# Cross attention in a decoder layer: where the weights are transposed and the values multiplied

## The reference, cut to what matters

```python
x = x + attn(layernorm(x), ...)
q = (queries @ Wq + bq)      # 16 heads of 64, queries = layernorm(x)
k = (keys @ Wk + bk)         # 154 context rows per batch
v = (values @ Wv + bv)
att = einsum('bhqd,bhkd->bhqk', q, k) / 8
att = att * attention_weights            # fside
att = where(attention_mask, -inf, att)
att = softmax(att)
out = einsum('bhqk,bhkd->bhqd', att, v)
x = x + (out @ Wo + bo)
x = x + ffn(layernorm(x), ...)           # top 2 of 8 experts, and a shared one
```

## Time and profile before

| | us |
|---|---|
| median of three runs | 585.82 |
| runs | 584.96 to 586.62 |
| profiled execution, first to last instruction (span) | 582.9 |
| TensorE busy | 562.7 |
| VectorE busy | 441.9 |
| ScalarE busy | 326.0 |
| GpSimd busy | 233.1 |

### The profile page before, as it was taken

One profiled execution on the slowest core, in us unless ns is written; L12 is line 12 of the kernel. 1 busy time (PEld: TensorE's weight loads), 2 busy tenths in 40 slices (PEclk: granted clock), 3 DMA queues, 4 the chain that ended last, 5 costly groups with the idle time before them and its releaser, 6 DMA issues.

```text
span 582.9 us, 11123 instructions
## 1 busy us (share of the span) xinstructions
PE 562.7 (97%) x3656; PEld 426.1 (73%) x3656; DVE 441.9 (76%) x838; ACT 326.0 (56%) x1005; POOL 233.1 (40%) x228
## 2 busy tenths in 40 slices
PE   8999999999999999999999999999999999999991
PEld 6547566788697978888788787878777776666661
DVE  3999999999886879958688679866677555656650
ACT  3632424368869796795976939715223245455220
POOL 1110110307580834387234671625235333353443
PEclk9999999999999999999999999999999999999997
DMA  8930004162741231423316107892645443344323
GB/s 301 347 101 2 1 1 172 45 217 91 274 155 65 100 119 45 173 74 93 127 37 218 65 20 230 270 390 87 181 111 90 67 64 58 53 70 61 54 29 35
DMA packets 36183, 68.37 MB, mean 117 GB/s; under 512 B 5504, under 2 KB 29024, under 8 KB 33632
## 3 DMA queue, kind: packets, MB, share of 16 engines
q1 hardware_dynamic: 28208, 57.99, 29.7%
q0 software_dynamic: 6784, 8.95, 9.5%
q10 hardware_dynamic: 1136, 0.73, 0.4%
HBM read 56.62 MB, written 15.25 MB: 123 GB/s over the span
## 4 chain that ended last, share of the span: by engine, by line
PE 58%; DVE 18%; DMA 9%; issue 7%; POOL 3%; ACT 2%; POOLq 1%; SPq 0%; DVEq 0%
PE pb L744 9%; PE pb L636 6%; DVE R L1140 6%; PE pb L499 6%; PE pb L601 6%; PE pb L549 6%; DMA out_dram<-R 5%; PE pb L565 5%; PE pb L778 5%; PE pb L516 4%; PE pb L648 3%; DVE R L1163 3%; DMA x<-in_x_dram 2%; DMA out_dram<-R,hidx 2%; PE pb L569 2%
## 5 line engine op out<-in xcount | busy, mean ns | idle before, releaser
L896 ACT ACTIVATE R<-R,mx 128x154 f32<-128x154 f32 x256 | 104.4, 415 | 0.2
L1761 POOL DMA_INDIRECT out_dram<-R x36 | 55.8, 1549 | 80.3 <-DMA out_dram<-R 33.9
L744 PE MATMUL pb<-R 128*128 x256 | 81.0, 459 | 0.0
L1022 ACT ACTIVATE R<-R 128x352 f32<-128x352 f32 x36 | 17.9, 497 | 91.6 <-DVE R L1572 80.3
L744 PEld LDWEIGHTS pb<-R 128*128 128x128 f32 x256 | 46.2, 190 | 20.4
L499 PE MATMUL pb<-xnT,wq 128*128 128x256 f32 x256 | 58.2, 383 | 0.0
L887 ACT ACTIVATE R<-pb,bq 128x256 f32<-128x256 f32 x64 | 30.1, 474 | 47.9 <-PE pb L499 47.8
L499 PEld LDWEIGHTS pb<-xnT,wq 128*128 128x128 f32 x256 | 47.7, 190 | 7.8 <-issue 1.2
L908 ACT COPY R<-pb 128x512 f32<-128x512 f32 x80 | 40.8, 614 | 18.4 <-PE pb L549 18.3
L1685 POOL DMA_INDIRECT xs_dram<-xn,pos x32 | 31.8, 993 | 47.3 <-DVE pos L1324 39.0
L896 ACT ACTIVATION_READ_ACCUMULATOR R<-R,mx 128x1 f32 x256 | 49.5, 193 | 0.0
(11 more groups left out here) (202 smaller groups left out, 1180.1 us busy)
## 6 DMA issues: line engine op xcount, KB each, us to landing
R<-in_fside_dram SPq DMA_DIRECT2D x16, 1232.0 KB, 5.5
R<-in_L_ffn_w_dram SPq DMA_DIRECT2D x16, 352.0 KB
R<-in_mask_dram SPq DMA_DIRECT2D x16, 308.0 KB, 2.9
R<-xs_dram SPq DMA_DIRECT2D x32, 129.0 KB, 2.1
KV<-in_ebias_dram SPq DMA_DIRECT2D x2, 1440.0 KB
out_dram<-x SPq DMA_DIRECT2D x4, 512.0 KB, 4.7
R<-in_L_ffn_w_dram SPq DMA_DIRECT2D x8, 256.0 KB, 4.5
x<-in_x_dram SPq DMA_DIRECT2D x3, 512.0 KB, 11.4
```

The lines of the kernel that those rows point to most:

```text
L744: ins = e.matmul(pb[:, u.i, 0:F], xsT[:, s % 2, k, :], ew13[:, bass.ds(w_reg[s] * 1408 + q * 704 + k * F, F)], start=(k == 0), stop=(k == 1))
L896: ins = e.activation(att[t % 3][:, h, :], att[t % 3][:, h, :], ACT.Exp, bias=mx[:, a4, 1, h:h + 1], accum_out=mx[:, a4, 2, h:h + 1])
L1761: e.indirect_dma_start(out=out, out_offset=bass.IndirectOffsetOnAxis(ap=to.bitcast(U32), axis=0), in_=rows, in_offset=None, compute_op=ALU ...
```

## The change

In passes 2 to 7 all 40 transposes of a unit's weights follow each other, and the value products of both halves are made in one go into four banks instead of two times four: half 0 goes to columns 0 to 255 and half 1 to 256 to 511 of the same bank. VectorE reads the four banks with two operations of 1024 elements instead of four of 512, and `combined` takes its blocks in the order 0, 1, 4, 5, 2, 3, 6, 7. The queries of the next unit are split: blocks 0 to 3 before the transposes, 4 and 5 between transposes and product, 6 and 7 behind the product and `turned`. ScalarE's order follows. In pass 7, which has no queries, the second block of `shared_out` stands between transposes and product. Pass 1 is as before, as is the last unit's work behind pass 7.

```diff
@@ -571,6 +571,40 @@
                         if r % 2:
                             ins.then_inc(full[u.i], 1)
 
+            def product_whole(u8):
+                b = u8 // 4
+                uses = [u for g in range(2) for u in bank.take_pair(("av", u8, g))]
+
+                def turned_in(hf, n):
+                    d = bank["pT", u8, hf, n // 2]
+                    w.wait_ge(free[d.i], d.drained)
+                    return pT[:, hf, n, :]
+
+                for hf in range(2):
+                    cols = slice(256 * hf, 256 * hf + 256)
+                    for n in range(8):
+                        u, to = uses[n // 2], 64 * (n % 2 ^ n // 4)
+                        w.wait_ge(free[u.e], u.empty)
+                        e.matmul(pb[to:to + 64, u.i, cols], vm[b][:, 8 * hf + n, :], turned_in(hf, n),
+                                 start=(hf == 0), stop=False)
+                for hf in range(2):
+                    cols = slice(256 * hf, 256 * hf + 256)
+                    for g in range(2):
+                        for r in (0, 2, 1, 3):
+                            u, to = uses[2 * g + r // 2], 64 * (r % 2 ^ g)
+                            ins = e.matmul(pb[to:to + 64, u.i, cols], vr[b][32 * r:32 * r + 32, 2 * hf + g, :],
+                                           turned_in(hf, 8 + g)[32 * r:32 * r + 32, :], start=False, stop=(hf == 1))
+                            if hf and r % 2:
+                                ins.then_inc(full[u.i], 1)
+
+            def weights_all_turned(u8):
+                for n in range(3):
+                    d = bank["con", B - 1, n]
+                    w.wait_ge(free[d.i], d.drained)
+                for hf in range(2):
+                    for k in range(5):
+                        weights_turned(u8, hf, k)
+
             def values(u8, between, amid=None, turning=None):
                 for n in range(3):
                     d = bank["con", B - 1, n]
@@ -595,8 +629,8 @@
                 for q in range(2):
                     u = bank.take(("wo", u8, q))
                     w.wait_ge(free[u.e], u.empty)
-                    for j in range(8):
-                        d = bank["av", u8, j // 4, j // 2 % 2, 0]
+                    for j in (0, 1, 4, 5, 2, 3, 6, 7):
+                        d = bank["av", u8, j // 2 % 2, 0]
                         w.wait_ge(free[d.i], d.drained)
                         ins = e.matmul(pb[:, u.i, 0:D], oT[:, j, q * P:(q + 1) * P], wo[:, j, :],
                                        start=(j == 0), stop=(j == 7))
@@ -689,12 +723,21 @@
                 scores(u8)
                 if u8 == 1:
                     queries(2, range(7))
+                    values(0, None, None, lambda: queries(2, range(7, 8)))
                 elif u8 < 7:
-                    queries(u8 + 1)
+                    queries(u8 + 1, range(0, 4))
+                    weights_all_turned(u8 - 1)
+                    queries(u8 + 1, range(4, 6))
+                    if u8 in (4, 6):
+                        place(u8 // 2 - 2)
+                    product_whole(u8 - 1)
+                    if u8 in BETWEEN:
+                        turned(*BETWEEN[u8])
+                    queries(u8 + 1, range(6, 8))
                 else:
-                    shared_out(*FILL[6])
-                values(u8 - 1, BETWEEN.get(u8), (lambda: place(u8 // 2 - 2)) if u8 in (4, 6) else None,
-                       (lambda: queries(2, range(7, 8))) if u8 == 1 else None)
+                    shared_out(*FILL[6], lambda: weights_all_turned(6))
+                    product_whole(6)
+                    turned(*BETWEEN[7])
                 if u8 - 1 in FILL and u8 < 7:
                     shared_out(*FILL[u8 - 1])
                 if gating is not None:
@@ -900,7 +943,7 @@
 
             def evacuate(u8, hf, lo, hi):
                 for i in range(4 if u8 else 0):
-                    d = bank["av", u8 - 1, hf, i // 2, i % 2]
+                    d = bank["av", u8 - 1, hf, i // 2, i % 2] if u8 == 1 else bank["av", u8 - 1, i // 2, i % 2]
                     w.wait_ge(full[d.i], d.filled)
                 for k in range(lo, hi):
                     u = bank["pT", u8, hf, k]
@@ -970,19 +1013,28 @@
             for u8 in range(1, NU):
                 t0, t1 = 2 * u8, 2 * u8 + 1
                 gating = u8 >= 3 and u8 % 2
-                if u8 < 7:
-                    queries(u8 + 1, range(7 if u8 == 1 else 8))
-                evacuate(u8 - 1, 0, 0, 5)
                 if u8 == 1:
+                    queries(2, range(7))
+                    evacuate(0, 0, 0, 5)
                     queries(2, range(7, 8))
-                evacuate(u8 - 1, 1, 0, 3)
-                if u8 in BETWEEN:
-                    normalise(*BETWEEN[u8])
-                if u8 not in BETWEEN:
+                    evacuate(0, 1, 0, 3)
                     exps(t0, range(0, 2))
-                evacuate(u8 - 1, 1, 3, 5)
-                if u8 in BETWEEN:
-                    turned(*BETWEEN[u8])
+                    evacuate(0, 1, 3, 5)
+                else:
+                    if u8 < 7:
+                        queries(u8 + 1, range(0, 4))
+                    evacuate(u8 - 1, 0, 0, 5)
+                    evacuate(u8 - 1, 1, 0, 5)
+                    if u8 < 7:
+                        queries(u8 + 1, range(4, 6))
+                    if u8 in BETWEEN:
+                        normalise(*BETWEEN[u8])
+                    else:
+                        exps(t0, range(0, 2))
+                    if u8 in BETWEEN:
+                        turned(*BETWEEN[u8])
+                    if u8 < 7:
+                        queries(u8 + 1, range(6, 8))
                 if u8 == 7:
                     exps(t0, range(0, 8))
                     exps(t0, range(8, 16))
@@ -1250,6 +1302,20 @@
                     e.tensor_tensor(oT[:, j:j + 2, :], pb[:, u.i:u.i + 2, 0:256],
                                     bvT[:, j:j + 2].rearrange("p (j a) -> p j a", a=1).broadcast_to([P, 2, 256]),
                                     ALU.add).then_inc(free[u.i], 1)
+
+            def product_whole(u8):
+                w.wait_ge(in_bv, 16)
+                d = bank["wo", u8 - 1, 1]
+                w.wait_ge(full[d.i], d.filled)
+                for g in range(2):
+                    u, v = bank["av", u8, g, 0], bank["av", u8, g, 1]
+                    w.wait_ge(full[u.i], u.filled)
+                    w.wait_ge(full[v.i], v.filled)
+                    e.tensor_tensor(
+                        oT[:, :, :].rearrange("p (f b) q -> p f b q", f=2)[:, :, 2 * g:2 * g + 2, :],
+                        pb[:, u.i:u.i + 2, :].rearrange("p b (f q) -> p f b q", f=2),
+                        bvT[:, :].rearrange("p (f b a) -> p f b a", f=2, a=1)[:, :, 2 * g:2 * g + 2, :].broadcast_to(
+                            [P, 2, 2, 256]), ALU.add).then_inc(free[u.i], 1)
 
             def attended(u8, qs=(0, 1)):
                 w.wait_ge(xbo.sem, xbo[u8])
@@ -1424,15 +1490,18 @@
                 for hs in heads_of(t0):
                     top(t0, hs)
                     if hs == (0, 8):
-                        product(6, 0)
+                        product_whole(6)
                 mask(t1, (0, H))
-                if u8 < 7:
-                    product(u8 - 1, 0)
+                if u8 == 1:
+                    product(0, 0)
                 if u8 in (4, 6):
                     place(u8 // 2 - 2)
                 if u8 < 7:
                     top(t1, (0, H))
-                product(u8 - 1, 1)
+                if u8 == 1:
+                    product(0, 1)
+                elif u8 < 7:
+                    product_whole(u8 - 1)
                 if gating is not None:
                     logits(gating)
                 if u8 == 7:
```

## The result

The changed kernel takes 597.43 us, the median of five runs (596.68 to 599.65), against 585.82 for the kernel before: a ratio of 1.0209, 95% interval 1.0192 to 1.0225. By the medians it is slower by 11.6 us. The forecast was 597.2.

A forecast was written before the change was run, and what follows sets the result against it. Two nearly equal bounds: TensorE's own work, and a loop ScalarE, VectorE, GpSimd, TensorE. Shifts through the passes reach +11.4: 582.9 + 11.4 = 594.3 us of span, plus 2.9 to the median, 597.2; range 589 to 601.

The forecast's parts named there:

- TensorE's work: Value products on TensorE, passes 2 to 7: fewer changes to 32-row tiles, -0.35 us a pass, -2.1 over six.
- Half 1 too early for GpSimd: Transposes wait for GpSimd's scaled second half: 1.4 us in pass 2, 1.4 in pass 3 (part earlier), 1.05 in pass 6.
- ScalarE's start: Exponentials stand behind queries 6 and 7: 1.9 us later every pass by order alone, 3.3 in pass 2 with its wait.
- Banks: TensorE waits for VectorE's first product operation to free banks: gate in pass 3 about 1.0 us, `shared_out` in pass 4 1.7.
- Pass 5: -0.35 us, then the gate chain again as in pass 3: a shift of +7.2 us at the scores of pass 6.
- Pass 7, the step that failed: VectorE's whole product comes between the halves of `top`, +11.6 us; +11.4 from the transposes of weights 7 to the end.
- Span to median: Whole kernel: the median of the runs lies 2.9 us above the profiled span, taking 594.3 to 597.2 us.
- Rival (a): Only ScalarE's order and pass 7 bite, no waits for scaled halves or banks: +5.7, 591.5 us; chance 0.21.
- Rival (c): Mask and `scale` swap order in passes 2 and 6, GpSimd takes 1.90 us, not 4.38: 594.8 us; chance 0.12.
- Rival (b): TensorE is the bound everywhere, hand-overs stay hidden, only row-tile changes count: -2.1, 583.7 us; chance 0.06.

The follow-up runs named there:

- the memsets: Changed kernel with three small memsets on VectorE before the even tile's mask in passes 2 and 6: 598.05 us, ratio 1.0218.
- the first experiment: Kernel before the change with only `turned` moved behind the second value product, so ScalarE's exponentials start 2.5 us later: 593.16 us, ratio 1.0127.
- queries 0 to 5: Changed kernel with query blocks 0 to 5 all ahead of the transposes: 594.99 us, ratio 1.0155.
- pass 7 with both blocks first: Changed kernel with both blocks of `shared_out` ahead of the 40 transposes in pass 7: 595.45 us, ratio 1.0165.

## Why the prediction was right, and where it was not

The mechanism and the size were right: 597.2 against 597.43, span +11.4 against +12.0. By its steps:

- **TensorE's work.** -0.35 a pass was right: 4.65 for a product where 4.70 was said, half of the tile-change stalls gone. VectorE's two operations take 2.35 together (2.2 said).
- **Half 1 too early for GpSimd.** Right in pass 2 (1.21, said 1.4) and 6 (0.79, said 1.05), and in pass 7 it is 0.93. In pass 3 it stands ahead of the queries, as 1.09. Moving two blocks of queries in front of the transposes takes both away (-2.4 us with what else it moves). GpSimd's operation was 4.38 us again, and the memsets showed that this comes from the mask that starts before it.
- **ScalarE's start.** The largest term: delaying it in the kernel before costs 7.5 us, and bringing four exponentials forward gives 2.3. Giving ScalarE its old order back together with all the rest gives 11, which does not single it out. The first exponential of pass 2 starts at 184.19 in ScalarE's timeline, 23.4 us after the scores at 160.80; before it was 20.0, so 3.4 more.
- **Banks.** The gate's and `shared_out`'s waits came at the size said. That they cost time is read from the trace; no run takes them away alone.
- **Pass 5.** The prediction's terms, 6.0 + 1.9 - 0.5, add up to 7.4; it wrote 7.2 "and rounding". Measured were 7.4.
- **Pass 7, the step that failed.** "VectorE has the whole product between the halves of `top`", and it was to wait for TensorE there. It did not: the change puts `shared_out`'s second block behind 40 transposes, and VectorE's own `shared_out` stands ahead of the mask. I moved VectorE's product by what TensorE does and overlooked that its mask hangs on that block. +13.0 instead of +11.6; taking the wait away gave 2.0 us. At the transposes of weights 7 this left +12.6 instead of +11.4. The span shows only +12.0, because the profiled execution after began pass 2 0.59 us earlier than the one before, which has nothing to do with the change.
- **Span to median.** Every run whose span is on record lies 1.8 us above it; the 2.9 that I added held 1.1 us of chance, as the profiled execution before was that much faster than the median. With 1.8 the forecast would have been 596.1 against the profiled execution's 596.68, which is in turn 0.75 below its own median. So the near hit at the median is in part luck: 0.6 and 0.75 too little, and 1.1 too much.

Rival (a) would have been 591.5: its terms were there, but not alone. Rival (c) did not happen by itself (mask ahead by 0.30 us), and when forced the time did not fall. Rival (b) is refuted by the first experiment: a delay of ScalarE of 2.5 us in a pass came back in full at `total(5)`.

The Trainium skill's port rule (SBUF — State Buffer, Who interferes with whom) has the first of the two engines hold the ports. The trace agrees, with 1.90 us for GpSimd and 4.23 for the mask where it had been 4.38 and 2.92.

## What to carry to other kernels

When work is moved on the busiest engine, follow what the other engines have queued behind its result: here two blocks of queries behind the product kept the exponentials waiting, and the new order as a whole cost about 11 us, five times the 2.1 us that the merged product takes off TensorE. A merged step frees its result only at its end, so the reader loses the first half it had before; it needs cover behind it. And when a block is moved past others, look for every reader of it, the engine with slack included.

## What the hardware showed

- When VectorE's mask and GpSimd's scaling overlapped here, they did not share the loss. The one that started first, by 0.3 us, took 1.90 us (GpSimd, as usual) or 2.92 (the mask, 2.72 alone), and the other took 4.38 instead of 1.90 or 4.23 instead of 2.72. That is nearly what is left of the first one plus the second's own time: 2.62 + 1.90 = 4.5 and 1.64 + 2.72 = 4.4 (estimates from these rows).
- Behind a stall of TensorE near 230 us (1.15 to 1.53 and 0.56 us) the granted clock fell to 0.50 for about 3 us in the profiled executions of three kernels (memsets, queries 0 to 5, delayed `turned`). It did not in two with the same stall (the kernel after, and pass 7 with both blocks first). The 32 rows of scores there took 3.97 to 4.04 us instead of 2.52. With one trace of each kernel it is not shown whether the kernel or the execution decides.
